# A two-layer cross-attention kernel: new row sums, a new path for half of the queries, and earlier first scores in the second attention

## The reference, cut to what matters

```python
q = (query @ Wq.T + bq).reshape(b, -1, 16, 8)       # query: layernorm(x)
k = (key @ Wk.T + bk).reshape(b, -1, 16, 8)         # key, value: the context
v = (value @ Wv.T + bv).reshape(b, -1, 16, 8)
attn = softmax(einsum('bqhd,bkhd->bhqk', q, k) / sqrt(8))
out = einsum('bhqk,bkhd->bqhd', attn, v).reshape(b, -1, 128)
x = x + tanh(g) * (out @ Wo.T + bo)
```

## Time and profile before

| | us |
|---|---|
| median of 3 runs (lowest, highest) | 272.99 (272.81, 273.55) |
| the profiled execution's own time | 273.14 |
| its span | 271.1 |

### The profile page before, as it was taken

The page is one execution under the profiler, slowest core; times in us unless marked ns, Lnnn a source line. Parts: engine busy times, 40 slices in busy tenths (PEclk is TensorE's granted clock), DMA queues, the critical chain, the costliest instruction groups (busy, mean ns, idle before and its releaser), DMA issues.

```text
span 271.1 us, 7236 instructions
## 1 busy us (share of the span) xinstructions
PE 247.6 (91%) x2956; PEld 210.0 (77%) x2956; DVE 190.0 (70%) x478; ACT 110.5 (41%) x187; POOL 69.6 (26%) x83
## 2 busy tenths in 40 slices
PE   8879989899999999989999998998798988879992
PEld 3558878788998888769999997997576877757881
DVE  1537798967365989896256586438788998879753
ACT  2565545544441554323134453430636454221220
POOL 2355393445433533340010031001122001111000
PEclk9999999999999999999999999999999999999998
DMA  6519600030000000598499100340052000000011
GB/s 200 188 45 321 175 1 4 2 157 4 0 2 2 1 2 7 87 147 308 189 169 171 49 0 0 118 116 1 2 174 63 2 2 5 0 0 4 8 30 41
DMA packets 14705, 18.98 MB, mean 70 GB/s; under 512 B 2384, under 2 KB 11472, under 8 KB 14544
## 3 DMA queue, kind: packets, MB, share of 16 engines
q1 hardware_dynamic: 14528, 18.26, 25.6%
q10 hardware_dynamic: 144, 0.26, 0.5%
HBM read 13.80 MB, written 4.72 MB: 68 GB/s over the span
## 4 chain that ended last, share of the span: by engine, by line
PE 66%; DVE 16%; issue 5%; DMA 4%; ACT 4%; POOL 2%; SPq 1%; DVEq 0%
PE OC L1130 9%; PE MB L1090 5%; PE MB L980 5%; PE SP L1051 5%; PE OC L1073 5%; PE TP L1060 4%; PE MB L982 4%; PE MB L981 4%; PE TP L1243 3%; PE MB L1202 2%; PE MB L1206 2%; PE OC L1079 2%; DMA w_raw<-in_w 2%; PE SP L982 2%; PE SP L980 2%
## 5 line engine op out<-in xcount | busy, mean ns | idle before, releaser
L398 POOL TENSOR_TENSOR S_sb<-S_sb,nmax 128x512 f32<-128x512 f32 x32 | 33.2, 1039 | 38.9 <-DVE nmax L701 38.9
L798 DVE SCALAR_TENSOR_TENSOR x_sb<-OC,gate,x_sb 128x128 f32<-128x128 f32 x64 | 18.0, 345 | 26.8 <-PE OC L1130 26.8
L1130 PEld LDWEIGHTS OC<-f_w,hid 128*128 128x128 f32 x256 | 30.9, 192 | 1.4
L692 DVE TENSOR_TENSOR S_sb<-SP,maskb 128x512 f32<-128x512 f32 x32 | 21.9, 686 | 13.5 <-PE SP L1051 13.3
L1130 PE MATMUL OC<-f_w,hid 128*128 128x128 f32 x256 | 31.0, 275 | 0.0
L701 DVE TENSOR_REDUCE nmax<-S_sb 128x4 f32<-128x512 f32 x32 | 22.0, 686 | 1.1
L507 ACT ACTIVATE PT<-TP 128x512 f32<-128x512 f32 x32 | 19.0, 593 | 7.8 <-PE TP L1060 7.7
L1060 PE MATMUL TP<-id_sb,S_sb 128*128 128x128 f32 x128 | 19.6, 275 | 2.4 <-POOL S_sb L398 2.4
L368 POOL TENSOR_SCALAR var_eps<-mv 128x4 f32<-128x4 f32 x8 | 2.0, 245 | 70.9 <-DVE mv L646 70.9
L1073 PE MATMUL OC<-PT,arena_f 128*32 128x128 f32 x512 | 17.6, 275 | 2.3 <-issue 1.7
L1060 PEld LDWEIGHTS TP<-id_sb,S_sb 128*128 128x128 f32 x128 | 14.9, 141 | 5.6 <-POOL S_sb L398 3.9
(11 more groups left out here) (187 smaller groups left out, 582.5 us busy)
## 6 DMA issues: line engine op xcount, KB each, us to landing
arena_f<-in_zeros SPq DMA_DIRECT2D x1, 2048.0 KB, 14.5
w_raw<-in_w SPq DMA_DIRECT2D x4, 384.0 KB, 4.0
k_dram<-f_r SPq DMA_DIRECT2D x3, 512.0 KB, 13.9
arena_r<-k_dram SPq DMA_DIRECT2D x4, 384.0 KB
arena_r<-q_dram SPq DMA_DIRECT2D x16, 96.0 KB
ew_raw<-in_f0w SPq DMA_DIRECT2D x1, 1024.0 KB, 6.0
f_w<-in_f0w SPq DMA_DIRECT2D x1, 1024.0 KB, 9.8
row_dram<-f_r SPq DMA_DIRECT2D x2, 512.0 KB, 3.1
```

Source lines behind the costliest of these rows:

```text
L398: g.tensor_tensor(S_sb[:, b], S_sb[:, b], nmax[:, b].unsqueeze(2).to_broadcast([P, H4, P]), ALU.add).then_inc(shifted, 1)
L692: v.tensor_tensor(S_sb[:, b].rearrange("p (r a) k -> p r a k", r=2), SP[:, :, 2 * P * b:2 * P * (b + 1)].rearrange("p r (a k) -> p r a k", ...
L1130: ins = mm(OC[:, n % 2, batch(t)], hid[:, n % 2, c, batch(t)], f0_w2[:, e, c, :], start=(c == 0), stop=(c == 1))
```

## The change

- **Earlier first scores.** `scores1(0, 0)`, `scores1(0, 1)`, `maxima1(0)` and `scores1(1, 0)` move into rounds 13 to 15 of feed-forward 0 on PE, with `max1(0, ·)` and `shift1(0)` as hooks on DVE. As `SP`, `TP` and `OC` are taken there, the first three tiles use both ring banks (`SPARE`).
- **Hooks of feed-forward 0.** The second half's normalisation, transposes and routing come one round earlier; `route_gates(0, 1)` moves from after `stats_of_sum(0)` in round 7 to round 6. `queries1(0)` moves on PE from ahead of `hidden0(12)` to ahead of `expert0(10)`.
- **Queries.** The four pattern rows now travel in the same DRAM tile, and `place_heads` is one DMA for each stretch, of 128 rows where the four had 96. The second half of the queries no longer goes through DRAM: for each of four row groups two multiplies with a selector (`spread_queries`) put them in place in PSUM, and ACT copies them into `q1s` (`place_queries`).
- **Sums.** The selector of `outputs1` is `row_of`, which puts each head's sum on one row. ACT copies output and sums to SBUF (`copy_outputs`), DVE turns the sums, takes a reciprocal of 16 columns, turns them back spread over 8 rows, and POOL does the product (for the last sequence DVE).
- **Fills.** `keep_clock` in `maxima1(0)` (24) and `fill_wait(3)` (6) go; `fill_wait(0)` has 20 instead of 16 dummy multiplies, `fill_wait(1)` 6 instead of 16.
- The 256 KB load of `col_sel_sb` goes; the order of rows in `Wv`, `bv` and `Wo` is changed on the host.

```diff
             def place_heads(dst, dram, moved):
+                sp.dma_start(dst.bitcast(F32), dram.rearrange("i p t -> p i t")).then_inc(moved, 16)
...
+            sp.wait_ge(q_sent, 48)
+            for w in range(2):
+                tok = slice(2 * P * w, 2 * P * (w + 1))
+                place_heads(q1s[:, :, tok], q_dram[:, :, tok], q_moved[w])
...
         @block.gpsimd
...
+            def normalise1(b):
+                pool.wait_ge(o_sum1, 3 * (b + 1))
+                g.tensor_tensor(oT1[:, batch(b)], o_sb[:, b % 2, 0:P], R1[:, b % 2], ALU.mult).then_inc(o_done1, 1)
...
         @block.scalar
...
+            def place_queries(i):
+                name = ("p", i)
+                wait_full(act, name)
+                sc.activation(q1s[:, i, half(1)], ring(name), ACT.Copy).then_inc(placed, 1)
...
+            def copy_outputs(b):
+                name = ("o", b)
+                wait_full(act, name)
+                if b > 1:
+                    act.wait_ge(o_done1, b - 1)
+                sc.activation(o_sb[:, b % 2], ring(name)[:, 0:2 * P], ACT.Copy).then_inc(o_copied, 1)
...
+            exp1(0, 0)
+            exp1(0, 1)
+            xnT_hi_copy(2, 1)
+            queries1(1)
+            exp1(1, 0)
+            exp1(1, 1)
+            for i in range(4):
+                place_queries(i)
+            hooks = {2: [lambda: split_f1(0), lambda: split_f1(1)], 3: [lambda: split_f1(2), lambda: split_f1(3)]}
+            for b in range(2, B):
                 for hook in hooks.get(b, ()):
                     hook()
+                if b < B - 1:
+                    copy_outputs(b - 2)
                 exp1(b, 0)
                 exp1(b, 1)
+            copy_outputs(B - 3)
+            copy_outputs(B - 2)
             xnT_hi_copy(3, 0)
+            copy_outputs(B - 1)
...
         @block.vector
...
             def normalise1(b):
+                dve.wait_ge(o_copied, b + 1)
+                v.transpose(sumT[:], o_sb[:, b % 2, P:2 * P].rearrange("p (c r) -> p c r", r=32)).then_inc(o_sum1, 1)
+                dve.wait_ge(o_sum1, 3 * b + 1)
+                v.reciprocal(rsum1[:], sumT[:, :, 0:4]).then_inc(o_sum1, 1)
+                dve.wait_ge(o_sum1, 3 * b + 2)
...
+                v.transpose(R1[:, b % 2].rearrange("p (c i d) -> p c i d", c=4, i=4),
+                            rsum1[:].unsqueeze(3).to_broadcast([P, 4, 4, DH1])).then_inc(o_sum1, 1)
...
+                     6: [lambda: route_gates(0, 1)], 7: [lambda: stats_of_sum(0)], 8: [lambda: normed(2, 0)],
+                     9: [lambda: xnT_lo_copy(2, 0), lambda: queries1(0)], 12: [lambda: max1(0, 0)],
+                     13: [lambda: max1(0, 1)], 14: [lambda: shift1(0)]}
...
             stats_of_sum(1)
+            max1(1, 0)
             normed(2, 1)
+            max1(1, 1)
+            xnT_lo_copy(2, 1)
+            shift1(1)
+            max1(2, 0)
+            queries1(1)
+            max1(2, 1)
...
         @block.tensor
...
+            def spread_queries(i):
+                name = ("p", i)
+                bank = take(name)
+                pe.wait_ge(pairs_done, 1)
+                pe.wait_ge(q1_los, 2)
+                rows = slice(32 * i, 32 * (i + 1))
+                mm(bank, head_sel[rows, 0], q1_hi[rows, :], start=True, stop=False)
+                done(name, mm(bank, head_sel[rows, 1], q1_lo[rows, :], start=False, stop=True))
...
-                        ins = mm(bank[rows, P:2 * P], col_sel_sb[:, i, rows], PT1[b % 3][:, j, i, :],
+                        ins = mm(bank[rows, P:2 * P], row_of[:, i, :], PT1[b % 3][:, j, i, :],
...
+            hooks = {0: [lambda: output0(1, 0)], 1: [lambda: output0(1, 1)], 4: [lambda: xn_transposes(1, 1)],
+                     5: [lambda: logits(0, 1)], 10: [lambda: xn_transposes(2, 0)], 14: [lambda: scores1(0, 1)],
+                     15: [lambda: maxima1(0), lambda: scores1(1, 0)]}
+            mid = {10: [lambda: queries1(0)], 13: [lambda: scores1(0, 0)]}
             for n in range(N0):
                 for hook in hooks.get(n, ()):
                     hook()
                 if n + 1 < N0:
                     hidden0(n + 1)
+                for hook in mid.get(n, ()):
+                    hook()
                 expert0(n)
+            scores1(1, 1)
+            turned1(0, 0)
+            turned1(0, 1)
+            fill_wait(0)
+            xn_transposes(2, 1)
+            maxima1(1)
+            scores1(2, 0)
+            scores1(2, 1)
+            queries1(1)
+            turned1(1, 0)
+            fill_wait(1)
+            turned1(1, 1)
+            for i in range(4):
+                spread_queries(i)
```

More of the change, by code:

```diff
@@ L73 @@
 USE = {name: k for k, name in enumerate(RING)}
-AREAS = [("s", 0, 0), ("s", 0, 1)]
-for seq in range(B):
+SPARE = [("s", 0, 0), ("s", 0, 1), ("t", 0, 0)]
+AREAS = [("s", 1, 0), ("s", 1, 1), ("t", 0, 1)]
+for seq in range(1, B):
     AREAS += [("s", seq + 1, 0), ("s", seq + 1, 1)] if seq + 1 < B else []
@@ L83, in build @@
           wqk1, bqk1, wv1, bv1, wo1, bo1, gw1, gb1, f1w13, f1w2,
-          ident, causal, k_rows, zeros, col_sel, pairs, rev0, rev1, out):
+          ident, causal, k_rows, zeros, pairs, rev0, rev1, out):
     with ExitStack() as ctx:
@@ L108, in build @@
         warm_sb = sb("warm_sb", [P, 512], BF16)
-        row_of = sb("row_of", [P, 2, 32])
+        row_of = sb("row_of", [P, 4, 32])
         tanh_g = sb("tanh_g", [P, 4])
@@ L267, in area_read, with wait_area, wait_queries @@
             return (maxed1 if kind == "s" else expd1), 2 * b + j + 1
+        def wait_area(eng, *name):
+            if name in SPARE:
+                for r in range(2):
+                    wait_full(eng, ("a", SPARE.index(name), r))
+            else:
+                eng.wait_ge(slot_full[AREA[name] % 3], AREA[name] // 3 + 1)
+        def wait_queries(eng, b):
+            if b < HB:
+                eng.wait_ge(q_moved[b // 2], 16)
+            else:
+                eng.wait_ge(placed, 4)
         block = ctx.enter_context(nc.Block())
@@ L338, in _ @@
             sp.wait_ge(v1_done, 2)
-            sp.dma_start(pair_raw, pairs).then_inc(in_pairs, 16)
+            sp.dma_start(sel_raw, pairs).then_inc(in_pairs, 16)
             sp.dma_start(f1_w2[:], f1w2.rearrange("e p n -> p e n")).then_inc(in_f1w2, 16)
[L341 to L350, removed]
+            sp.wait_ge(q1_his, 1)
+            send_heads(q_dram, 0, q1_hi[:], q_sent)
+            send_heads(q_dram, 1, q1_hi[:], q_sent)
+            sp.wait_ge(q1_los, 1)
+            send_heads(q_dram, 2, q1_lo[:], q_sent)
+            sp.wait_ge(q_sent, 48)
+            for w in range(2):
+                tok = slice(2 * P * w, 2 * P * (w + 1))
+                place_heads(q1s[:, :, tok], q_dram[:, :, tok], q_moved[w])
             ot = out.rearrange("b t d -> t b d")
@@ L413, in _ @@
             pool.wait_ge(consts, 4)
-            for b in range(2):
+            for b in range(4):
                 const(row_of[:, b, b:b + 1], 1.0)
@@ L925, in _ @@
             stats_of_sum(1)
-            dve.wait_ge(consts, 6)
-            max1(0, 0)
-            max1(0, 1)
+            max1(1, 0)
             normed(2, 1)
-            early = {1: [lambda: queries1(1)]}
-            mid = {0: [lambda: xnT_lo_copy(2, 1)], 7: [lambda: residual(1, 0, 0), lambda: residual(1, 0, 1),
+            max1(1, 1)
[4 more added lines that the diff above has]
+            max1(2, 1)
+            mid = {7: [lambda: residual(1, 0, 0), lambda: residual(1, 0, 1),
                                                        lambda: stats_after(3, 0)]}
             late = {7: [lambda: normed(3, 0)]}
-            for b in range(B):
+            for b in range(2, B):
                 shift1(b)
-                for hook in early.get(b, ()):
-                    hook()
                 if b + 1 < B:
@@ L991, in fill_wait @@
                 name = ("w", b)
-                done(name, keep_clock(take(name)[:, 0:256], 16 if b < 2 else 6))
+                done(name, keep_clock(take(name)[:, 0:256], (20, 6)[b]))
             def xn_transposes(n, h):
```

210 lines of the change are left out of this document (97 added, 113 removed).

## The result

| | before | after |
|---|---|---|
| median of 20 runs | 274.0 | 276.3 |
| lowest, highest | 272.75, 280.74 | 273.12, 284.7 |
| profiled execution | 273.14 | 277.33 |
| its span | 271.1 | 275.5 |

The changed kernel is slower by 0.7%: ratio 1.0068, 95% interval 1.0038 to 1.0098. The forecast of 271.1 and its range both missed, on the side given 11%. Ratios leave out executions over 1.5% above the fastest of their kernel, the profiled one of the changed kernel (277.33) among them; medians don't. So a few tenths between two groups say little. The mean clock of an execution is the granted clock averaged over it, 1.00 being 2.4 GHz.

What follows compares the result with a forecast made beforehand. PE, busy 91% of the span at full clock, bounds the kernel, so gains come from its waits. 1.7 through attention 1 plus 0.2 from the sums take 1.9 off 273.14: 271.2, or 271.1 for the median; range 269.5 to 273.3.

Steps and rivals of the forecast that it cites:

- step 5: Removed load, POOL fills, selector copy, keys' placing and fewer dummy multiplies in attention 1: all counted at nothing.
- The clock rival: Attention 1: PE's thin stretch E+9.9 to E+12.8 drops the clock to 1.2 GHz, 2.0 us slower, 275.0; 11%.
- E: The moment the last feed-forward multiply ahead of attention 1 ends: 184.43 before, forecast 186.5.
- Step 1: Feed-forward 0: earlier hooks remove PE's 1.19 us wait ahead of the transposes; net 1.0 us gained.
- Step 2: First scores inside feed-forward 0: 2.1 us of PE work moved there, plus a 1.0 us wait for placed queries.
- Step 3: Attention 1: second half of the queries without DRAM brings sequence 4's turned scores to E+24.6 from E+28.4, 3.8 us gained.
- Step 4: Attention 1's sums: nothing gained in the loop on PE, DVE, ACT or POOL; 0.2 us gained at the end.
- The transfer rival: Feed-forward 0: slow sending and placing DMAs make the first scores wait 3.45 us, leaving no gain, 273.5; 17%.
- Theory B: From the experiments: the new way through attention 1 is simply longer, so time stays above before's at full clock too.

Runs made afterwards that it cites:

- fill: The changed kernel plus 14 dummy multiplies, between the second and third spread pair and after the fourth: 272.62, ratio 0.9981.
- best: both with 30 instead of 20 dummies in `fill_wait(0)`, and 3 each behind the transposes and ahead of `queries1(1)`: 271.57, ratio 0.9951.
- hooks: The kernel before with only the hooks of feed-forward 0 moved as in the change, and `queries1(0)` with them: 272.91, ratio 0.9976.
- both: The changed kernel with the 14 dummies of fill and the exponential's table loaded early, behind the last SiLU: 271.27, ratio 0.9928.
- dram_best: best with the second half of the queries sent through DRAM again: 272.9, ratio 0.9962.
- old_sums: fill with the kernel before's sums: DVE reciprocal of 128 columns and product, no ACT copy, no POOL product: 273.0, ratio 0.9976.
- late: both with first scores and maxima behind feed-forward 0 again, under 34 dummy multiplies: 277.41, ratio 1.0139.
- control: The changed kernel again, with no edit: 274.8, ratio 1.0076.
- table: The changed kernel with the exponential's table loaded early by a one-column exponential behind the last SiLU: 275.81, ratio 1.0122.

## Why the prediction was wrong

**The step that failed** is the last sentence of step 5, that the dummy multiplies go from 62 to 26, "which frees nothing by itself, as they filled waits", with what rests on it: every wait of PE was priced at its own length, and the clock was left to a rival at 11%. The sentence is true of the path and leaves out what the dummies did for the clock. thin shows it by removing 59 from the kernel before, after which no execution kept its clock; fill and best show it by adding 14 and 30 (best with the early table load besides): now some executions of fill and most of best kept theirs, and these were faster than the kernel before.

**The clock rival was the right one, in part.** It put a fall behind the spread pairs, near E+12.8, as sequence 2's maxima wait. It came at 199.5, E+13.8, behind two of the pairs, and cost 2.4, not 3.9: the outputs of sequence 0 took 3.6 (202.39 to 205.96) where fill has 1.9, 1.7 more, which is most of it. The rival missed two more places: the wait of 1.24 ahead of the 20 dummies (1.7) and feed-forward 1 (2.4), which the change doesn't touch. Hence 275.0 in place of 277.3 for the profiled execution. The prediction argued against it that the clock had held through a wait of 1.19, and that no longer one is seen. The second is misread: the kernel before waits longer in attention 1, ahead of 16 dummies, and holds its clock there too:

```profile
196.77 1.92 PE L987 MATMUL MB<-warm_sb 128*128 128x256 bf16 x16 [1.29 <-DVE q_lo L827]
```

So the length of one wait does not decide. In the changed kernel waits of 0.60 and 1.24 stand ahead of the first fall, and 0.78 and 1.07 between it and the second, with fewer dummies between them. The Trainium skill says under "TensorE: Matmul & The Clock Gate", "HAM oscillation — how this bites in real kernels", that an engine left waiting comes back at half rate. The rows agree on the half rate, 0.50, but show it in the changed kernel behind waits of 1.24 us and less, and not in every execution.

**The accounts of the profiled executions**, by the start of PE's last multiply: before 266.07, at full clock (fill) 264.57, so 1.50 gained; falls 1.67 + 2.36 + 2.38, and 0.07 at E, so 271.05, 4.98 later than before. The spans say 2.1 gained and 6.5 lost, 4.4 slower; the 0.6 between the two accounts lies behind the last multiply, up to the end of the writing out of the result, which no step touches.

**The steps at full clock**, in fill:
- Step 1: right. No wait ahead of the transposes; the profile of hooks measures 0.8 to 1.0 for 1.0.
- Step 2: the 2.1 of PE work is there; the wait of 1.0 for the placed queries is not. In the changed kernel's profile the low part left at 168.88 (169.15 was forecast), landed 3.2 later, and the placing DMA landed in 4.1, not 4.7. E is 185.6, not 186.5: 0.9 better.
- Step 3: `queries1(1)` starts at E+7.4, near the forecast, and the first spread pair at E+10.0 for E+9.9, but sequence 4's exponential starts at 211.25, E+25.6 and not E+24.6. The table load was not in the sum; at full clock both, where it is out of the way, has the same spans. E is 0.9 early and the rest 1.0 late, so the two errors cancel, by luck: 212.87 - 211.25 = 1.6 gained for 1.7. And the 3.8 that the step put down to the new path are not its worth, since dram_best goes through DRAM and has the same spans.
- Step 4: right that it is worth nothing in the loop. The copy took 0.38 for 0.4, the turnings and the reciprocal 0.87 together, the period stays at 4.25. The 0.2 gained at the end does not show: old_sums is as fast.
- The transfer rival (17%) is out: the first scores did not wait.

DVE in a loop of the changed kernel, for step 4:

```profile
215.21 0.31 DVE L896 STREAM_TRANSPOSE sumT<-o_sb 128x128 f32<-128x128 f32 x1 [0.47 <-ACT o_sb L582]
215.55 0.25 DVE L898 RECIPROCAL rsum<-sumT 128x16 f32<-128x16 f32 x1
215.84 0.31 DVE L902 STREAM_TRANSPOSE R<-rsum 128x128 f32<-128x128 f32 x1
```

**What stays open**: what decides, in one execution, whether the clock falls; why the clock falls again in feed-forward 1; what the early scores are worth by themselves, since late was no clean test. Theory B falls: at full clock the changed path is the shorter one, 268.8 to 269.5 of span for 270.5 to 271.1.

## What to carry to other kernels

Before you take dummy multiplies or a long wait out of PE's stream, read its busy time and granted clock microsecond by microsecond, and put a few dummy multiplies into each short wait that is left, in an area nobody uses. Compare two kernels by their executions at the same granted clock first, to see what the edit does, and only then by the median, which also counts how often each one falls. An equal mean clock is not an equal cost, though: at 0.965 to 0.966 thin took 273.9 to 274.4, and at 0.966 to 0.967 the changed kernel took 276.8 and more. What a fall costs depends on who waits for PE while it lasts. An early table load or a shorter transfer is worth only what the next wait leaves of it.

## What was not expected of the hardware

- The clock fell from 1.00 to 0.50 in a stretch whose longest wait was 1.24 us (185.7 to 199.5 us in the changed kernel), and it held through one of 1.29 in the kernel before. And the same instructions do not fall in every execution: fill's twelve range from a mean clock of 1.00 to 0.979.
- In all five profiles where the clock was still low at 203 us (after, control, table, both, thin), it fell once more in feed-forward 1, beginning 41 us after it had come back (206.3 to 247.3, 204.6 to 245.5, 204.0 to 244.9, 207.1 to 248.2, 203.2 to 244.2). In the nine others it did not, though PE's waits there, 0.98, 0.70 and 0.79, are the same within 0.01 in fill and in the changed kernel. This fall costs 2.4 us, and its cause is not known from these runs.
- A table load can stand behind the wait of the instruction that needs it (186.42 here, after 4.58 us of idle time), and so be on the path although its engine had time before.
